# Two finals of each set behind the scales, a split power, a pair-wise end: one gated block on one core

## The reference, cut to what matters

```
x = x + tanh(g_xattn) * (ctx @ Wv @ Wout + bout)
h = layernorm(layernorm(x)) * ln1_g + ln1_b      # 256 wide
h = act_quant(h) @ weight_quant(w1).T + b1       # to 1024, 8-bit rows, ternary weights
h = gelu(h)
h = layernorm(h) * ln2_g + ln2_b                 # 1024 wide
h = act_quant(h) @ weight_quant(w2).T + b2       # back to 256
x = x + tanh(g_ffn) * h
```

## Time and profile before

| | us |
|---|---|
| median of 3 runs | 356.12 (355.98 to 356.35) |
| the profiled execution | 356.32 |
| its span, first to last instruction | 354.5 |
| PE busy | 296.9 (84%) |
| DVE busy | 294.9 (83%) |
| ACT busy | 277.2 (78%) |
| POOL busy | 265.2 (75%) |
| mean granted TensorE clock | 0.957 of full |

### The profile page before, as it was taken

The page is one execution under the profiler, slowest core; times in us unless marked ns, Lnnn a source line. Parts: engine busy times, 40 slices in busy tenths (PEclk is TensorE's granted clock), DMA queues, the critical chain, the costliest instruction groups (busy, mean ns, idle before and its releaser), DMA issues. The chain is left out here.

```text
span 354.5 us, 5862 instructions
## 1 busy us (share of the span) xinstructions
PE 296.9 (84%) x1680; PEld 191.7 (54%) x1704; DVE 294.9 (83%) x521; ACT 277.2 (78%) x444; POOL 265.2 (75%) x298
## 2 busy tenths in 40 slices
PE   5998887889898979898989899989998849394566
PEld 4867463537475646465656565655655424242344
DVE  0268898989999999999999999989999948666582
ACT  2155696898989899998989898989898977779340
POOL 4045789997989888989898989898898986738410
PEclk9999999989999999999999999999999978978598
DMA  7956513364858685768666767595555445361457
GB/s 220 324 188 252 151 61 89 118 150 119 189 131 182 111 204 138 170 157 145 182 154 159 160 164 152 165 150 150 112 97 106 104 95 114 74 133 38 82 115 213
DMA packets 98634, 51.57 MB, mean 145 GB/s; under 512 B 87097, under 2 KB 89588, under 8 KB 98602
## 3 DMA queue, kind: packets, MB, share of 16 engines
q1 hardware_dynamic: 97706, 51.15, 59.5%
q10 hardware_dynamic: 896, 0.04, 0.2%
HBM read 21.79 MB, written 8.41 MB: 85 GB/s over the span
## 5 line engine op out<-in xcount | busy, mean ns | idle before, releaser
L395 POOL TENSOR_TENSOR y<-u,g_bc 128x1024 f32<-128x1024 f32 x64 | 151.0, 2368 | 15.3 <-ACT u L572 14.3
L776 DVE TENSOR_TENSOR y<-y,slot_c 128x1024 f32<-128x1024 f32 x64 | 77.7, 1214 | 23.3 <-PE slot_c L1070 23.3
L780 DVE TENSOR_REDUCE amax<-y 128x1 f32<-128x1024 f32 x64 | 78.0, 1218 | 1.8
L553 ACT ACTIVATE q<-y,scale 128x1024 f16<-128x1024 f32 x64 | 70.0, 1144 | 8.2 <-DVE scale L811 8.2
L580 ACT ACTIVATE junk<-u,usum 128x1024 bf16<-128x1024 f32 x64 | 73.7, 1151 | 2.0
L1112 PE MATMUL bank_f<-w2T,q2T 128*128 128x256 f16 x448 | 60.7, 281 | 7.4 <-DVE res L823 5.5
L1112 PEld LDWEIGHTS bank_f<-w2T,q2T 128*128 128x128 f16 x448 | 44.6, 101 | 23.5 <-DVE res L823 6.1
L1028 PE MATMUL slot_a<-wvo,ctxT 128*128 128x256 f32 x208 | 53.4, 386 | 1.0 <-ACT ctxT L515 1.0
L1070 PE MATMUL slot_c<-ln_rows,rows 128*128 128x512 bf16 x119 | 38.1, 397 | 16.6 <-ACT rows L563 7.2
L572 ACT ACTIVATE u<-slot_a,d 128x1024 f32<-128x1024 f32 x32 | 35.5, 1109 | 10.8 <-PE slot_a L1099 9.3
L1028 PEld LDWEIGHTS slot_a<-wvo,ctxT 128*128 128x128 f32 x208 | 36.3, 190 | 11.1 <-ACT ctxT L515 3.6
(11 more groups left out here) (136 smaller groups left out, 430.9 us busy)
## 6 DMA issues: line engine op xcount, KB each, us to landing
c_in<-in_ctx SPq DMA_DIRECT2D x16, 512.0 KB, 4.2
x_in<-in_x SPq DMA_DIRECT2D x16, 512.0 KB, 4.1
out<-res SPq DMA_DIRECT2D x31, 256.0 KB, 2.5
y<-in_L_ffn_w SPq DMA_DIRECT2D x2, 1024.0 KB, 9.0
u<-in_L_xattn_Wkv SPq DMA_DIRECT2D x2, 512.0 KB, 6.2
u<-in_L_xattn_Wout SPq DMA_DIRECT2D x2, 512.0 KB, 7.4
q2T<-q SPq DMA_TRANSPOSE x64, 3.3
g_bc<-in_L_ffn_ln_g SPq DMA_DIRECT2D x1, 512.0 KB, 5.5
```

The lines of the kernel that those rows point to most:

```text
L395: nc.gpsimd.tensor_tensor(y[:, k % 3, t, :], u[:, t, :], g2_bc[:, :], ALU.mult).then_inc(gain2_done, 1)
L553: nc.scalar.activation(q2[:, t, :], y[:, k % 3, t, :], ACT.Copy, scale=scale[:, (k + 1) % 2, 1, t:t + 1]).then_inc(q2_done, 1)
L776: nc.vector.tensor_tensor(line, line, slot_c[:, :], ALU.add).then_inc(y_done, 1)
L780: nc.vector.tensor_reduce(amax[:, 1, t:t + 1], y[:, k % 3, t, :], AX.X, ALU.max, apply_absolute_value=True).then_inc(amax2_done, 1)
```

## The change

It has many parts, listed here by place.

- Scales (DVE): the factor 127 * 2^-24 (STEP) is folded in, a separate lower bound goes; six instructions become five.
- POOL: root becomes root_first (norm 1, directly after norm_first) and root_second (norm 2). variance issues its first instruction before it waits for the squares.
- Finals 0 and 1 of set i-3 stand at the head of DVE's body i, where they were those of i-2 ahead of the scales; finals 2 and 3 stand singly between rows; join stands after row 0. Body S-1 keeps its finals ahead of the scales. SP's store(i-3, 0) follows turn_second(i-2, 1).
- PE: ctx transposes between correction 1 and hidden 1; hidden 2 and 3 ahead of correction 3 and of the second product of tile 0; the second product of tile 1 ahead of the attention. Where no attention is left, 14 dummy products into slot_a at the end of the body, and 2 ahead of turn_rows in bodies S-2 and S-1.
- ACT: the second take_context between gelu 2 and square 2.
- End: bodies go to S+2; POOL takes the variance and power of set S-1 for tiles 0, 1 and for tiles 2, 3 apart, and turn_rows runs once more.
- Start: Wv and Wout are loaded in four pieces each, copied by DVE and ACT in turns; 22 warm-up products wait only for a memset on DVE; the loads after them are in another order.

```diff
@@ POOL, root and variance
-                def root(j):
-                    wait(pool, var1_done, min(j + 2, S))
-                    ...
-                    nc.gpsimd.tensor_tensor(rstd[:, j % 2, :, :], var[:, :, :], half_neg[:, :, :],
-                                            ALU.pow) \
+                def root_first(k):
+                    wait(pool, var1_done, k + 1)
+                    wait(pool, scales_ready, scales_after(k - 3))
+                    nc.gpsimd.tensor_tensor(rstd[:, (k - 1) % 2, 0, :], var[:, 0, :],
+                                            half_neg[:, 0, :], ALU.pow).then_inc(root1_done, 1)
+                def root_second(j):
+                    ...
+                    nc.gpsimd.tensor_tensor(rstd[:, j % 2, 1, :], var[:, 1, :], half_neg[:, 1, :],
+                                            ALU.pow).then_inc(rstd_done, 1)
@@ def variance(k)
+                    wait(pool, gelu_done, T * k + T)
+                    wait(pool, split_steps, split_count(i))
+                    nc.gpsimd.tensor_scalar(stat[:, 2, :], usum[:, :], -1.0 / H, None, ALU.mult)
                     wait(pool, square_done, T * k + T)
                     wait(pool, std_done, i + 2)
-                    wait(pool, split_steps, split_count(i))
-                    nc.gpsimd.tensor_scalar(stat[:, 2, :], usum[:, :], -1.0 / H, None, ALU.mult)
@@ POOL, last bodies
+                if i == S - 1:
+                    gain(S - 2, 3)
+                    gain(S - 1, 0)
+                    gain(S - 1, 1)
+                    pair_root(0)
+                    return
+                if i == S:
+                    pair_root(1)
+                    return
+                if i == S + 1:
+                    gain(S - 1, 2)
+                    gain(S - 1, 3)
+                    return
@@ SP
-                if live(i - 2):
-                    turn_second(i - 2, 0)
                 if live(i + 4):
                     load_x(i + 4)
                 if live(i - 2):
+                    turn_second(i - 2, 0)
                     turn_second(i - 2, 1)
                 if live(i - 3):
+                    store(i - 3, 0)
                     store(i - 3, 1)
+                if live(i - 2):
+                    turn_second(i - 2, 2)
+                if i == S - 1:
+                    store(i - 2, 0)
                 if live(i + 5):
                     load_context(i + 5)
-                if live(i - 2):
-                    turn_second(i - 2, 2)
-                    store(i - 2, 0)
@@ DVE
+                if live(i - 3):
+                    final(i - 3, 0)
+                    final(i - 3, 1)
                 if live(i + 2):
                     residual(i + 2, 0)
 ...
-                if live(i - 2):
+                if i == S - 1:
                     final(i - 2, 0)
                     final(i - 2, 1)
                 if live(i + 1):
                     scales()
@@ PE
+                def keep_warm(n, first=False):
+                    wait(pe, gelu_done, T * (i - 1) + 3 if first else T * min(i, S - 1) + 3)
+                    for _ in range(n):
+                        nc.tensor.matmul(slot_a[:, 512:1024], ident_b[:, :], b1_rows[:, 0, 0:512],
+                                         start=True, stop=True)
 ...
+                if live(i + 3):
+                    attention(i + 3, 1)
+                else:
+                    keep_warm(14)
@@ ACT
                     gelu(2)
+                if live(i + 3):
+                    take_context(i + 3, 1)
+                if live(i):
                     square(2)
```

More of the change, by code:

```diff
@@ L203, in product_bank @@
             if k == S - 2:
[L204 to L208, removed]
+                return (bank_q[:, 0:D], slot_a[:, 0:D], bank_q[:, D:2 * D], slot_a[:, D:2 * D])[t]
+            return (slot_a[:, 512:512 + D], bank_f[:, 0:D], slot_b[:, 0:D], slot_b[:, 512:512 + D])[t]
+        bodies = range(-3, S + 3)
         def split_count(i):
@@ L330, in _ @@
             turn_second(S - 3, 3)
-            for t in range(T):
-                turn_second(S - 2, t)
-            for t in range(T):
-                turn_second(S - 1, t)
+            turn_second(S - 2, 0)
+            turn_second(S - 2, 1)
+            turn_second(S - 2, 2)
+            turn_second(S - 2, 3)
             store(S - 3, 1)
+            turn_second(S - 1, 0)
+            turn_second(S - 1, 1)
+            turn_second(S - 1, 2)
             store(S - 2, 0)
+            turn_second(S - 1, 3)
             store(S - 2, 1)
@@ L382, in gain_first, with pair_deviations @@
+                def pair_deviations(h):
+                    two = slice(2 * h, 2 * h + 2)
+                    wait(pool, rstd_done, S + h)
+                    nc.gpsimd.tensor_tensor(stat[:, 3, two], var[:, 1, two], rstd[:, S % 2, 1, two],
+                                            ALU.mult).then_inc(std_done, 1)
                 def gain_first(k):
@@ L791, in scales @@
                     wait(dve, amax2_done, T * (i - 1) + those.stop)
[L792 to L795 removed]
+                    wait(dve, root1_done, min(i + 2, S))
+                    wait(dve, rstd_done, i + (those.stop > 2 and i == S))
+                    wait(dve, split_steps, split_count(i + (i == S)))
@@ L815, in final @@
+                    nc.vector.scalar_tensor_tensor(
+                        out=scale[:, i % 2, kinds, those], in0=amax_inv[one], scalar=STEP / QEPS, in1=power,
+                        op0=ALU.min, op1=ALU.mult).then_inc(scales_ready, 1)
                 def final(k, t):
-                    if k == S - 1:
-                        wait(dve, ffn_done, T * k + (t + 1 if t > 1 else 2))
+                    if k == S - 2:
+                        wait(dve, ffn_done, T * k + T)
+                    elif k == S - 1:
+                        wait(dve, ffn_done, T * k + t + 1)
@@ L907, in body @@
                     row(i - 1, 1)
+                if live(i - 3):
+                    final(i - 3, 2)
+                if live(i - 1):
                     row_max(i - 1, 1)
-                if i == S:
-                    scales(slice(1, 2), slice(0, 2))
+                    row(i - 1, 2)
+                if live(i - 3):
+                    final(i - 3, 3)
                 if live(i - 1):
-                    row(i - 1, 2)
                     row_max(i - 1, 2)
@@ L1209, in body @@
                     correction(i - 1, 2)
+                if live(i):
+                    hidden(2)
+                    hidden(3)
+                if live(i - 1):
+                    correction(i - 1, 3)
                 if live(i - 2):
```

346 lines of the change are left out of this document (194 added, 152 removed).

## The result

The changed kernel takes 335.82 us (median of 4 runs, 335.26 to 336.33) against 356.24 for the one before in the same runs (355.98 to 356.75): ratio 0.9425 with an interval of 0.9405 to 0.9445. The forecast was 339.5 with a range of 333 to 349. The profiled execution took 336.33, its span is 334.4 where it was 354.5: 20.1 us less.

What follows compares the result with a forecast made beforehand. No engine alone bounds it; a loop of waits through POOL closes without slack. Steady bodies 3.6, next periods 1.0 and 3.2, end 6.7 and start 2.3 sum to 16.8 us won: forecast 339.5 us, range 333 to 349.

Steps and rivals of the forecast that it cites:

- This loop: PE's closed loop from shift through turn_rows to the fourth row: 17.63, taken as 17.8 a body, winning 3.6 us.
- The chain through POOL: Square-to-rows chain in steady bodies: 18.02 less 0.28 and 0.74, plus 0.56 for the context copy, makes 17.56.
- Rival (a): POOL's 4-column power costs the same 1.67 as 8 columns, so POOL sets 18.4 a body: 352.3 us; chance 0.12.
- The scales: DVE's scales: five instructions save 0.20, moved finals bring them about 1.1 us earlier, ACT's 0.85 idle closes.
- The store's move: SP's queue: store(i-3,1) stands before turn_second(i-2,2), about 5 us later than its data, 5 us left: costs nothing.
- Last full bodies: Bodies 13 to 15, no attention left: dummy products keep the clock, periods 17.1, winning 1.0 and 3.2 us.
- Rival (b): The end stays cold: 2.3 in the second period, 2.4 in body 15, 2 in the products: 346 us; chance 0.14.
- The end: Set 15's tail: last quantising 24.4 after the rows copy, then 13.6 unchanged; 38.0 against 44.7, winning 6.7 us.
- The start: Up to the rows copy at 71.97: earlier combining, smaller power and scales win 2.3 us, bounds -1 to 5.
- Rival (c): Denser waits drop PE's clock in the steady bodies, 2.5 a body; in 11 of them 367 us; chance 0.04.
- Rival (d): Loops looser than drawn (power under 0.93, second square order helps): 17.5 a body, 333 us; chance 0.04.
- The signs: Expected in the profile: copies 17.7 to 17.8 apart, power near 0.93, clock near 1 from 271 to 310, first gelu near 38.9.

Runs made afterwards that it cites:

- a4: Kernel after, with PE's second product of tile 1 and its bias moved ahead of the first-layer shift: 332.55 us, ratio 0.934.
- a5: Kernel after, with ACT's copy of the second context half put back behind the last square: 336.27 us, ratio 0.9436.
- a2: Kernel after, with one 8-column power on POOL in place of two of 4 columns: 341.66 us, ratio 0.9596.
- b2: Kernel before, with only POOL's part: power split in two of 4 columns, the first and the sum ahead of the last square's wait: 353.67 us.
- c1: Kernel after, with finals 0 and 1 and their store back ahead of the scales, but the context load issued ahead of that store: 340.62 us.
- b1: Kernel before, with only finals 0 and 1 and their store moved behind the scales, context load staying where it was: 355.25 us.
- a3: Kernel after, without the dummy products (neither the 14 nor the 2): 338.46 us, ratio 0.9504.
- b3: Kernel before, with only the dummy products added (2 ahead of turn_rows, 14 at the end of the last bodies without attention): 355.12 us.
- a1: Kernel after, with finals 0 and 1 and their store back ahead of the scales, nothing else: 366.76 us, ratio 1.028.
- c2: Kernel after, with only the 512 KB context load moved to directly ahead of the fourth transpose of the next pass: 343.33 us.
- a9: a4 plus two tail edits: SP's last fourth transpose ahead of a store, and filling products between the last set's corrections: 332.71 us.

## Why the prediction was right, and where it was off

The sum, 16.8, was 3.3 short of 20.1. The eleven steady periods alone were 3.9 short; the start was 0.3 short, the last two periods 0.2 and the end 0.7 too much.

- *The step that was mis-sized: "This loop ... is 6.8 + 1.39 + 9.44 = 17.63. I take 17.7 and add 0.1 for hiccups: 17.8 a body."* The loop was the right one: after the change PE's queue is last at turn_rows (0.39 behind POOL), the shift waits for the fourth row (0.54), and a4, which changes only this loop, goes to 17.19. Its size is 17.49. (The terms of any closed loop add up to the period, so that sum is no proof; a4 is.) Of the 0.35 between 17.8 and the measured mean of 17.45, 0.14 is the loop itself (shift to turn_rows 6.73, turn_rows to the first row 1.38, from there to the next shift 9.38, which is 17.49; 0.04 of the difference is the fourth row, taken as 1.25 where the earlier trace rows have 1.21), 0.07 my rounding up, 0.1 hiccups that I carried over and that did not come, and 0.04 the shorter first and last of the eleven. Times eleven: 3.9.
- *The chain through POOL.* Predicted 17.56 with a power of 0.93. It took 1.04, which by that sum makes 17.67; but POOL still had 0.39 to spare at turn_rows, so the chain was 17.10. The term that was too large is the context copy, put at 0.56: from rows copy to the end of the last square ACT took 13.31 (174.15 to 187.46) for 13.25, with the copy in it, and 12.97 in a5 without it. So the copy costs 0.34, and the rest of the stretch is 0.28 shorter than before. Splitting the power is worth 0.40 a body in the kernel after (a2), but only 0.13 in the one before (b2). Rival (a), a power that costs 1.67 however few its columns, is out. So is the price by which half the columns cost about half, 0.84: 1.04 is 0.62 of 1.67. (The Trainium skill, "GPSIMD Engine Reference", has the loop and the dispatch in the section "Instruction dispatch"; that the bound is the number of elements stands in "Elementwise — side-by-side cycle accounting".)
- *The scales.* "The 0.85 idle closes": to 0.35. "Without the move of the finals the scales would end near the time POOL wants to split, and cost 0.2 a body": c1, where the store moves back too, shows 0.33. But in the kernel before the same move is worth nothing (b1). The two parts belong together.
- *The store's move, priced at "nothing".* Right for where it was put. What the text did not see is what the queue is worth: put back with the finals it costs 28.1 us of span, since the context load and the transposes follow it, and 4.3 when the load goes first (c1).
- *Last full bodies.* 0.9 and 3.1 for 1.0 and 3.2, the clock at 1.00 as argued; a3 and b3 show that the dummy products do it (2.0 and 2.3 in that period). Rival (b) is out for the bodies.
- *The end.* The quantising at 320.09 came 24.33 after the copy, for 24.4. From there it took 14.3, not 13.6: the bound "2 us more if PE is cold when set 14's products come" did happen (1.91 for eight). Against a4, whose profiled tail is at full clock, it cost 0.7 (38.64 for 37.9): PE, once warm, waits 1.78 for a transpose, so most of it was covered. That tail is not a4's merit, as the last section shows.
- *The start.* 2.6 for 2.3; nothing was tried on its parts, so the near hit bears out none of them.
- Rival (c), a clock that falls from denser waits, did not come in the kernel after. In a1 it came in five of nine bodies, and these take 1.6 more than the other four; but these four, at clock 1.00, are at 19.4 to 20.0 also slower than before. The waits there are those of 1.6 to 2.2 for a transpose, not those for rows that I had named.
- Rival (d), looser loops at 17.5 and 333 us, had the pace exactly. It got 0.04. I had it as a separate case, though it was the low end of my own loop. Its time does not follow from its pace: 11 x 0.3 below 339.5 is 336.2.
- *The signs.* The clock stayed at 1.00 until 315, the quantising came at 24.33, the first row waited 0.24. The first gelu came at 38.18 for 38.9. POOL's wait for the square was 0.60, not near 0.3, and the copies were 17.49 apart, not 17.7 to 17.8: POOL's chain and PE's loop were both shorter than drawn.

## What to carry to other kernels

When two chains meet at one operation and close at nearly one length, each edit alone measures as little (b1 and b2: 0.01 and 0.13 a body) and both together as 0.48: judge them by the pace in undisturbed periods, together. In a queue that serves transposes on the path, look at what stands directly ahead of them and what it waits for: a store that waits for a late result, with a large load behind it, cost far more (28.1 of span) than the one without the other (4.3 and 7.1). And give a loop the sum of its rows, not that sum rounded up on every body.

## What the runs showed of the hardware

- POOL's power takes 1.67 us for 8 columns, 1.04 for 4 and 0.72 for 2 (in the tail of the kernel after), which is 0.16 a column on top of 0.4, where its other 4- and 8-column operations take 0.19 to 0.31.
- The clock's fall in the tail comes and goes. The kernel after and a4 have nearly the same waits there (PE 1.30, 0.81 and 1.43 us for DVE's rows; 1.29, 0.81 and 1.43) and the same code, and yet the clock fell to 0.59 in one and stayed at 1.00 in the other. Between the last two rows copies it is 0.69 in the kernel after and c1, 0.83 in a2, a5 and c2, and 1.00 in a1, a4 and a9; all but a9 have the same tail. From the third-last rows copy to the end it is 23.7 and 23.8 at 0.69, and 22.9 to 23.0 in a1, a2, a4, a5 and c2. So the 0.7 that a4 gains there does not belong to its edit. What decides the fall stays open.
- A transpose issued 0.4 to 0.8 us behind a 512 KB load let PE start 4.4 us (c2), 4.6 and 4.85 us (a1) after its issue, and PE had waited for it. With the load 4.5 us ahead, in the kernel after, PE started 4.0 after the issue without a wait, and with the load 5.3 us ahead, in c1, 3.4 after it.
- The small DVE operation that took 2.07 us at the start while POOL multiplied is met again after the change: another instruction of the same scales takes 2.12 us where it takes 0.12 in the loop, and it ends at 46.65, with POOL's multiplies (41.83 to 46.62). DVE's timeline, then POOL's:

```profile
44.53 2.12 DVE L875 SCALAR_TENSOR_TENSOR d<-amax_g,deq 128x8 f32<-128x8 f32 x1
```

```profile
41.83 4.79 POOL L433 TENSOR_TENSOR y<-u,g_bc 128x1024 f32<-128x1024 f32 x2
```

In the loop the scales run at 188.12 to 188.80 under the power (187.81 to 188.85) and take 0.12 to 0.20 each. The rule of the Trainium skill, "SBUF — State Buffer", section "Who interferes with whom", by which a DVE instruction with two inputs in SBUF contends with a GpSimd instruction that reads SBUF, agrees with the first and not with the second.
